# Relative-position attention: relative stores, bias loads and output stores on GpSimd's queue, relative products at a head's last step, transposes three steps behind

## What is computed

```
Q, K, V = x @ Wq.T, x @ Wk.T, x @ Wv.T          # as (b, h, s, 8)
scores = Q K^T / sqrt(8)
dist = clip(k - q, -128, 128) + 128
scores = scores + einsum('bhqd,qkd->bhqk', Q, pek[dist]) / sqrt(8)
scores = where(causal, scores, -inf)
attn = softmax(scores)
out = attn V + einsum('bhqk,qkd->bhqd', attn, pev[dist])
return merged(out) @ Wo.T
```

## Time and profile before

| | us |
|---|---|
| median of 3 runs (4418.83 to 4434.67) | 4421.69 |
| the profiled execution | 4445.3 |
| its span, first to last instruction | 4443.5 |
| TensorE busy in it | 2959.2 (67%) |
| VectorE busy | 2377.8 (54%) |
| ScalarE busy | 1767.3 (40%) |
| GpSimd busy | 809.7 (18%) |

### The profile page before, as it was taken

One profiled execution on the slowest core, in us unless ns is written; L12 is line 12 of the kernel. 1 busy time (PEld: TensorE's weight loads), 2 busy tenths in 40 slices (PEclk: granted clock), 3 DMA queues, 4 the chain that ended last, 5 costly groups with the idle time before them and its releaser, 6 DMA issues. The chain is left out here.

```text
span 4443.5 us, 68068 instructions
## 1 busy us (share of the span) xinstructions
PE 2959.2 (67%) x21547; PEld 1611.6 (36%) x21547; DVE 2377.8 (54%) x4808; ACT 1767.3 (40%) x4259; POOL 809.7 (18%) x1093
## 2 busy tenths in 40 slices
PE   5588734285443678777887577877777630768885
PEld 2344323154332344444444333333333320752221
DVE  4566466454674566666664344445544441137775
ACT  2355412121111455545554244444444300227675
POOL 2100000021001444444442300000000007022220
PEclk9789866587665899999998666666666655879998
DMA  3422110000001000000000477777777514663331
GB/s 112 76 53 50 40 43 0 8 1 6 0 0 43 19 15 18 18 18 17 10 18 9 140 189 188 189 194 194 189 190 197 135 41 142 169 133 53 58 56 38
DMA packets 457690, 340.63 MB, mean 77 GB/s; under 512 B 64351, under 2 KB 418842, under 8 KB 457378
## 3 DMA queue, kind: packets, MB, share of 16 engines
q1 hardware_dynamic: 434562, 302.49, 27.9%
q0 software_dynamic: 11008, 27.28, 2.1%
q10 hardware_dynamic: 11808, 7.08, 0.6%
HBM read 174.71 MB, written 146.81 MB: 72 GB/s over the span
## 5 line engine op out<-in xcount | busy, mean ns | idle before, releaser
L1156 DVE TENSOR_REDUCE a_soft_NM<-a_soft_s_ps 128x2 f32<-128x1024 f32 (+3 forms) x512 | 515.2, 1021 | 235.3 <-PE a_soft_s_ps L1091 133.3
L1190 ACT ACTIVATE a_soft_PTS<-a_soft_st_ps 128x512 f32<-128x512 f32 (+3 forms) x1024 | 458.9, 523 | 173.5 <-PE a_soft_st_ps L1067 101.9
L465 PE MATMUL a_soft_pt_ps<-net_ident,a_soft_PR 128*128 128x128 f32 x1280 | 328.2, 369 | 116.1 <-ACT a_soft_PTS L567 110.4
L613 ACT ACTIVATE a_soft_PR<-a_soft_s_ps,a_soft_least 128x128 f32<-128x128 f32 (+3 forms) x512 | 263.6, 526 | 341.3 <-DVE a_soft_least L588 227.1
L1062 PE MATMUL a_soft_st_ps<-a_soft_QS,a_soft_KS 50*128 50x512 bf16 (+4 forms) x1024 | 263.0, 365 | 72.8 <-ACT a_soft_PTS L1190 40.7
L465 PEld LDWEIGHTS a_soft_pt_ps<-net_ident,a_soft_PR 128*128 128x128 f32 x1280 | 182.7, 180 | 214.7 <-ACT a_soft_PR L613 154.6
L1104 PE MATMUL a_soft_o_ps<-a_soft_PTS,a_soft_VR 128*32 128x512 f32 (+3 forms) x2048 | 249.5, 562 | 0.1
L2212 PE MATMUL f_run_ps<-f_run_WQKV,f_run_HT 128*128 128x512 f32 x384 | 229.5, 689 | 15.5 <-DVE f_run_RS L1433 8.3
L2545 ACT ACTIVATE f_run_PB<-f_run_ps,f_run_MX 128x128 f32<-128x128 f32 x512 | 179.8, 377 | 136.6 <-DVE f_run_MX L2427 136.6
L2350 POOL TENSOR_TENSOR f_run_QK<-f_run_QK,f_run_T 128x512 f32<-128x512 f32 x128 | 163.2, 1275 | 366.4 <-DVE f_run_T L2405 363.9
L569 DVE COPY a_soft_PTS<-a_soft_pt_ps 128x512 f32<-128x512 f32 (+3 forms) x320 | 169.4, 529 | 69.3 <-PE a_soft_pt_ps L465 42.2
(11 more groups left out here) (376 smaller groups left out, 6473.5 us busy)
## 6 DMA issues: line engine op xcount, KB each, us to landing
a_soft_BIAS<-skew_d SPq DMA_DIRECT2D x256, 191.0 KB, 4.2
band_d<-a_soft_PR SPq DMA_DIRECT2D x256, 191.0 KB, 3.7
skew_d<-a_soft_RS SPq DMA_DIRECT2D x128, 256.0 KB, 4.4
a_soft_PB<-band_d SPq DMA_DIRECT2D x128, 256.0 KB, 3.1
f_run_W<-in_L_ffn_w SPq DMA_DIRECT2D x72, 256.0 KB, 2.7
a_soft_QS<-query_rows_d SPq DMA_DIRECT2D x32, 384.0 KB
query_rows_d<-a_proj_PARTS SPq DMA_DIRECT2D x72, 128.0 KB
query_rows_d<-a_proj_PARTS POOLq DMA_DIRECT2D x72, 128.0 KB
```

The lines of the kernel that those rows point to most:

```text
L465: last = pe.transpose(pt_ps[:, slot, kb * P:(kb + 1) * P], PR[:, n % NPR, OFF + kb * P:OFF + (kb + 1) * P], ident[:])
L613: act.activation(PR[:, n % NPR, OFF:OFF + width(j)], s_ps[:, n % 4, 0:width(j)], ACT.Exp, bias=least[:, n:n + 1], scale=-1.0).then_inc(pro ...
L1156: dve.tensor_reduce(NM[:, T % 2, j, p, :], s_ps[:, ring["s", a] % 2, :, 0:width(j)], AX.X, ALU.max, negate=True).then_inc(max_ready, 1)
L1190: act.activation(PTS[:, T % 2, 2 * p + par, kb, q0:S], st_ps[:, e % 3, q0:S], ACT.Exp, scale=scale).then_inc(probs_ready, 1)
```

## The change

The relative store, the bias loads and the output stores move to GpSimd, with the waits that stand ahead of them; SyncE keeps the operand loads and the band. TensorE makes the relative products in step j = 3 instead of j = 0, between the scores and the transposes; ScalarE copies them last in step j = 3 instead of first in j = 1, and no longer issues the output stores. Rows are transposed three steps behind instead of two (`LAG`). The counts of the semaphores follow (`missing`, `before`, `through`).

```diff
@@ relative_heads @@
+    LAG = 3
     def missing(seq, slots):
-        return sum(m < seq and m % 2 in slots for m in (0, 1, 2, 7))
+        return sum(m < seq and m % 2 in slots for m in (0, 1, 2, 3, 7))
     def before(hd, pos):
...
-        return 5 * hd + pos - 4
+        return 5 * hd + pos - 5
@@ sync @@
-            def store_rel(hd, h, visit):
-                sp.wait_ge(rel_copied, hd + 1)
...
-            def load_bias(hd, h, visit):
...
                 for h in range(4):
...
-                    for f, a in ((store_rel, 3), (load_bias, 2)):
-                        if not (final and h + a >= 4):
-                            f(hd + a, (h + a) % 4, qd if h + a < 4 else qd + 1)
                     store_band(hd, h, qd)
@@ gpsimd @@
+            def store_rel(hd, h, visit):
+                pool.wait_ge(rel_copied, hd + 1)
+                if not (isinstance(hd, int) and hd < 4):
+                    pool.wait_ge(bias_loaded[h], 16 * len(BIAS_WINDOWS) * visit)
+                pool.sem_inc(pool_passed, 1)
+                pool.dma_start(diagonal(skew_d, h), RS[:, h, :, :]).then_inc(rel_stored[h], 16)
+            def load_bias(hd, h, visit):
+                pool.wait_ge(rel_stored[h], 16 * (visit + 1))
+                pool.sem_inc(pool_passed, 1)
+                if not (isinstance(hd, int) and hd < 4):
+                    pool.wait_ge(least_ready, 4 * (hd - 3))
+                pool.sem_inc(pool_passed, 1)
+                for r0, n, c0, m in BIAS_WINDOWS:
+                    pool.dma_start(BIAS[r0:r0 + n, h, :, c0:c0 + m], window(skew_d, h, r0, n, c0, m)).then_inc(bias_loaded[h], 16)
...
+                for h in range(4):
+                    hd = 4 * qd + h
+                    if not (final and h >= 2):
+                        load_bias(hd + 2, (h + 2) % 4, qd if h < 2 else qd + 1)
+                    if not (final and h >= 1):
+                        store_rel(hd + 3, (h + 3) % 4, qd if h < 1 else qd + 1)
+                if prev:
+                    store(qd - 1, 1 - u % 2, *((b, u - 1) if u else (b - 1, 3)))
+            def store(qd, sl, b, u):
+                pool.wait_ge(o_copied, qd + 1)
+                for h in range(4):
+                    pool.dma_start(out_d[ds(b, 1), 4 * u + h].rearrange("a r f -> (a r) f"),
+                                   OS[32 * h:32 * h + HD + 1, sl, :]).then_inc(o_stored[sl], 16)
@@ tensor @@
-                    if j == 0 and not (final and h >= 1):
+                    if j == 3 and not (final and h >= 1):
                         uu, hh = (u, h + 3) if h < 1 else ((u + 1) % 4, h - 1)
                         relative(b if h < 1 or u < 3 else b + 1, uu, hh, 4 * qd + h + 3)
...
-                    if n >= 2:
-                        turn(qd, n - 2, h, pos, qd)
+                    if n >= LAG:
+                        turn(qd, n - LAG, h, pos, qd)
                     elif prev:
-                        turn(qd - 1, n + 14, h, pos, qd)
+                        turn(qd - 1, n + 16 - LAG, h, pos, qd)
@@ scalar @@
                     if prev or n >= NPR:
-                        act.wait_ge(pt_ready, before(4 * qd + h - 2, 4 + j))
+                        act.wait_ge(pt_ready, before(4 * qd + h - 2, (5, 6, 7, 9)[j]))
...
-                    if j == 1 and not (isinstance(b, int) and qd == 4 * B - 1 and h >= 1):
-                        copy_rel(4 * qd + h + 3, (h + 3) % 4, qd if h else qd - 1)
...
                     copies(act, 1, qd, sl, n, prev)
+                    if j == 3 and not (isinstance(b, int) and qd == 4 * B - 1 and h >= 1):
+                        copy_rel(4 * qd + h + 3, (h + 3) % 4, qd if h else qd - 1)
...
-                act.wait_ge(o_copied, qd + 1)
-                bb, uu = (b, u - 1) if u else (b - 1, 3)
-                for h in range(4):
-                    act.dma_start(out_d[ds(bb, 1), 4 * uu + h].rearrange("a r f -> (a r) f"),
-                                  OS[32 * h:32 * h + HD + 1, sl, :]).then_inc(o_stored[sl], 16)
```

More of the change, by code:

```diff
@@ L361, in load @@
                     sp.dma_start(t[:, sl, :], src[ds(b, 1), :, u * 4 * S:(u + 1) * 4 * S].rearrange("a p f -> (a p) f")).then_inc(opnd_loaded[sl], 16)
-            def store_rel(hd, h, visit):
-                sp.wait_ge(rel_copied, hd + 1)
-                if not (isinstance(hd, int) and hd < 4):
-                    sp.wait_ge(bias_loaded[h], 16 * len(BIAS_WINDOWS) * visit)
-                sp.dma_start(diagonal(skew_d, h), RS[:, h, :, :]).then_inc(rel_stored[h], 16)
-            def load_bias(hd, h, visit):
-                sp.wait_ge(rel_stored[h], 16 * (visit + 1))
-                sp.sem_inc(sp_passed, 1)
-                if not (isinstance(hd, int) and hd < 4):
-                    sp.wait_ge(least_ready, 4 * (hd - 3))
-                for r0, n, c0, m in BIAS_WINDOWS:
-                    sp.dma_start(BIAS[r0:r0 + n, h, :, c0:c0 + m], window(skew_d, h, r0, n, c0, m)).then_inc(bias_loaded[h], 16)
             def store_band(hd, h, visit):
@@ L397, in _ @@
             load(0, 0)
-            for hd in range(3):
-                store_rel(hd, hd, 0)
-            sp.wait_ge(init_done, 1)
-            for hd in range(2):
-                load_bias(hd, hd, 0)
             def quad(b, u, prev):
@@ L432, in _ @@
             pool.drain()
+            def store_rel(hd, h, visit):
[12 more added lines that the diff above has]
+                    pool.dma_start(BIAS[r0:r0 + n, h, :, c0:c0 + m], window(skew_d, h, r0, n, c0, m)).then_inc(bias_loaded[h], 16)
+            for hd in range(3):
+                store_rel(hd, hd, 0)
+            for hd in range(2):
+                load_bias(hd, hd, 0)
             def quad(b, u, prev):
                 qd = 4 * b + u
+                final = isinstance(b, int) and qd == 4 * B - 1
                 if not (isinstance(b, int) and qd < 2):
@@ L440, in quad, with last @@
                                  vall[:, ds(qd, 1), :, :].rearrange("p a h (j d) -> p (a h) j d", d=HD)).then_inc(vr_ready, 1)
-            batches(quad, lambda: None, pool)
+                for h in range(4):
[11 more added lines that the diff above has]
+                                   OS[32 * h:32 * h + HD + 1, sl, :]).then_inc(o_stored[sl], 16)
+            def last():
+                store(4 * B - 1, 1, B - 1, 3)
+                for o in o_stored:
+                    pool.wait_ge(o, 64 * 2 * B)
+            batches(quad, last, pool)
         def q_blk(sl, h, j):
@@ L528, in last @@
             def last():
[L529 to L530 removed]
+                turn(4 * B - 1, 13, 0, 0, 4 * B)
+                turn(4 * B - 1, 14, 0, 1, 4 * B)
                 turn_band(4 * B - 1, 2, 0, 4 * B)
[L532 removed]
+                turn(4 * B - 1, 15, 0, 3, 4 * B)
+                turn_band(4 * B - 1, 3, 0, 4 * B, 4)
                 for kb in range(NPT):
[L534 removed]
+                    pv(4 * B - 1, 1, kb, (1, -1))
             for hd in range(3):
@@ L641, in last @@
             def last():
-                copy_out(act, 1, 4 * B, 0, 1, 1, 3, 15)
-                copy_out(act, 1, 4 * B, 0, 3, 1, 3, None)
-                store(4 * B - 1, 1, B, 0)
-                for o in o_stored:
-                    act.wait_ge(o, 64 * 2 * B)
+                copy_out(act, 1, 4 * B, 0, 1, 1, 3, 14)
+                copy_out(act, 1, 4 * B, 0, 3, 1, 3, 15)
+                copy_outputs(4 * B - 1, 1, B, 0)
             for hd in range(3):
```

27 lines of the change are left out of this document (12 added, 15 removed).

## The result

The changed kernel takes 4444.7 us at the median (4436.6 to 4458.6, 9 runs) against 4421.7 for the kernel before: 1.0049 of its time, 95% interval 1.0034 to 1.0064, so 23 us or half a per cent slower. The forecast was 4340. The stage is where it is lost: the exponentials took 944.6 us and take 962.9 now, 18.3 us more. (The profiled execution of after, 4436.6 us, is the shortest of its nine and that of before, 4445.3, lies above all of its own, so the two spans differ the other way; what lies outside the stage is 3498.9 us in that of before and 3472.0 in that of after. So stages are compared in the traces and ratios in the runs.)

What follows compares the result with a forecast made beforehand. SyncE's queue was taken to bound the kernel at 29.6 us a quad. Afterwards GpSimd's 26.4 us a quad, 32 times, plus 17 for loop turns gave 862 against 944.6 us, 82 less: 4340 us, range 4260 to 4480.

Steps and rivals of the forecast that it cites:

- SyncE's loop bound the stage and loses its 2.04 us a head: SyncE's queue in the exponentials' stage: its 7.0 to 7.1 us turn falls to about 5.1 us a head.
- well above 17.8 + 7 us: Sign in the profile after: SyncE's band stores wait this long for exponentials, with band loads under 6.8 us apart.
- The engines take 25.7 us a quad without their two waits: TensorE's quad without waits for ScalarE (1.72 us) and operands (1.47), both said to be removed by the change: 25.7 us.
- The lag and the late products cost zero: Three-step lag and moved relative products: zero taken, up to 20 us of gain left in the range.
- Price of GpSimd's issues, 3.0 us for three: GpSimd's relative store and two bias loads per head: 3.0 us, the middle of 1.6 per issue and 4.4 per run.
- The landing, 3.8 us: GpSimd's relative store lands in 3.8 us, 3.4 behind the issue, as only SyncE's band transfers compete.
- Nothing gained: Rival, chance 0.16: SyncE's queue full but not in the way, landings stretch; 4395 to 4445 us, say 4420.
- about 7.3 if only half the stores meet it: GpSimd's loop per head if only half the stores meet the 5.4 us landing; 8.2 at worst.
- GpSimd's loop is longer than SyncE's was: Rival, chance 0.17: issues priced per run make GpSimd's loop 8.0 us a head, 78 us more, 4500 us.
- The lead of 10.4 us against 13.2: Relative product's way from copy to landed bias takes 10.4 us; VectorE wants it two heads later, 13.2 us: enough.
- The clock: Rival, engines and clock, chance 0.22: less idle time raises TensorE's clock, 1 us a quad; about 4285 us.
- The Trainium skill's two rules: Spreading issuing engines saves only issue time, gain near nothing; GpSimd transfer costs 2.0 us plus bytes, 2.6 for the store.

Runs made afterwards that it cites:

- the swapped order and the late band: Changed kernel with GpSimd's relative store ahead of its bias loads and the band transposed in step j = 3 instead of j = 2; 4368.3 us, 0.9863.
- 0.9891: Changed kernel with relative store ahead of bias loads, relative products back in step j = 0, band transposed in j = 3; 4374.0 us.
- 1.0068: Kernel before with relative stores, bias loads and outputs on GpSimd, but early relative products and a lag of two steps; 4501.9 us.
- either cut of bytes: Changed kernel, after four heads moving one block of four: of the band's stores and loads, 4359.0 us, 0.9856; or of the bias loads, 4350.0 us, 0.9835.
- the late band: Alone: changed kernel with only the band transposed in a head's step j = 3 instead of j = 2; 4473.1 us, 1.0103.
- the early products: Changed kernel with only the relative products back in step j = 0, copied in j = 1; 4463.9 us, 1.0076.
- two edits: On the changed kernel: relative store ahead of bias loads alone, 4457.3 us, 0.9977; band transposed in j = 3 alone, 1.0103; both, 0.9863.

## Why the prediction was wrong, point by point

- **SyncE's loop bound the stage and loses its 2.04 us a head: right.** The loop was there, and SyncE now waits for exponentials, which I had named as the sign. I wanted those waits "well above 17.8 + 7 us"; they are 307. But band loads are 7.35 and 7.63 us apart, not under 6.8: the queue is idle, not faster.
- **The engines take 25.7 us a quad without their two waits: not reached.** The kernel with the swapped order and the late band has 891.8 / 32 = 27.9, with bias waits in it. Both waits went (no operand row, no "issue" row), so their causes were rightly named, but the step "both waits have a reason that the change removes", as a gain, fails: the output stores alone gave 0.3% the wrong way, since the time came back as operand wait.
- **The lag and the late products cost zero: borne out on two queues.** Late products help by 0.27% at most on the order of the change and on the swapped one by nothing that the intervals tell (0.9863 against 0.9891), but with one queue they hold up the band. The lag is the only difference between 1.0068 and 1.0076, two ratios that their intervals don't tell apart.
- **Price of GpSimd's issues, 3.0 us for three: too high.** They take 2.0, nearer the end priced per issue (1.6) than that per run (4.4). By itself this would have made the kernel faster than forecast, so it hid 1.0 us of what the other terms were short. I had written that the change loses when the issues cost over 3.8 us; it lost with 2.0.
- **The landing, 3.8 us: the step that failed.** The landing is 5.5 us from the issue's start and 4.7 behind its end, where I had 3.8 and 3.4. The 0.2 "for waits" is 0.74, the time from the landing to the next issue, which no row of before had shown for GpSimd. So the sum 3.4 + 3.0 + 0.2 = 6.6 should have been 4.7 + 2.0 + 0.74 = 7.5: plus 1.3 for the landing, plus 0.5 behind it, minus 1.0 for the issues. 0.9 x 128 = 115 us, about the 105 between 4340 and 4445. I took the store to compete "only" with SyncE's band. It stands right behind 382 KB of bias loads of its own queue, in an order that the diff shows, and meets the band too; cutting either brings it to 4.4 and 4.5, and another place in the queue and in the head to 4.2. And the 3.2 us of the earlier trace rows were SyncE's; GpSimd's own first stores took 4.3.
- **The rivals: both of the losing ones had a part of it.** "Nothing gained" (chance 0.16) had the stretch of the landings, and its range ends at 4445, where the time came. But its "about 7.3 if only half the stores meet it" is near 7.5 by luck: it counts the issues at 3.0, and with the 2.0 measured it is 6.3, so that it took nearly the full stretch and the 0.74. "GpSimd's loop is longer than SyncE's was" (0.17) had the place and the sign: the loop is 7.52 against 7.39 us, (7.52 - 7.39) x 128 is about the 18 us lost in the stage, and VectorE waits for the bias in most heads. Its price, 4.4 us for the issues, was wrong.
- **The lead of 10.4 us against 13.2: wrong.** It took each store to go out when its copy was done. In the order of the change it stands behind the bias load, which waits for the landing of the store ahead. The product copied by 3106.75 us was stored at 3112.87, its bias loads went out at 3119.25, and VectorE's step that needs them started at 3124.40, after 1.29 us of waiting for them: 17.6 us. Whoever had followed that one product through the queue would have seen that the order, not the sum, was wrong.
- **The clock: no part in it.** The granted clock is 0.67 before and 0.66 after; it is 0.69 or 0.70 in the fastest kernels, where TensorE is busy 83 to 85% of the view and not 79%.
- **The Trainium skill's two rules.** The trace of before gives no landing of a store that GpSimd issued. The runs show 4.3 us near the start and 5.5 in the stage, so the fixed cost plus bytes that the Trainium skill gives in DMA: Bandwidth & Descriptors, section Anatomy of one DMA (2.6 us for this store, an estimate), is too short here by 1.7 to 2.9. The section Issuing engines are not separate DMA queues of the same page of the Trainium skill came nearer than my sum, in its outcome: nothing was gained. What the move saved SyncE is indeed the issues, as that section says; but it calls them usually small beside the transfer, and here they are 2.04 us of a loop of 7.1 whose landing is waited for. The runs with the swapped order and the late band reach 0.9863 with the same two queues and the same bytes, so sharing the DMA engines didn't rule out a gain.

**Still open:** why the store lands later from GpSimd than from SyncE even with little beside it; why either cut of bytes takes away the whole stretch; why the late band costs 0.5% while GpSimd's loop binds, and why the store lands 0.2 to 0.3 us later there and with the early products; what a loop turn costs now, which no run singled out.

## What to carry to other kernels

A store whose landing the same queue waits for is a loop, and its length is issues plus landing, plus the time from the landing to the next issue, whichever engine issues; moving it to an idle engine moves the loop. Before such a move, follow one piece of data through the new queue's order, and put what waits for an engine ahead of what waits for a landing, so that the landing passes while the queue waits anyway. When a first limit is taken away, try the next ones together: here two edits were worth 0.7% and minus 0.5% alone, and 1.9% together.

## What the runs showed of the hardware

- GpSimd issues by shape, but far from in proportion: 0.76 us for 128 rows of four runs of 512 B, 0.625 for 64 rows of four runs of 764 B, and 0.52 for an output store (2.07 / 4). SyncE takes 0.39 for the first and about 0.6 for the second.
- The same store of 256 KB lands in 3.2 us from SyncE and 4.3 from GpSimd with little else running, and in 4.4 and 5.5 in the stage, counted from the issue's start: 1.1 us apart both times, 0.4 of it the longer issue. For the query rows in the projection it is the other way round, 3.7 from SyncE and 3.0 from GpSimd.
- GpSimd issues the waiting bias load 0.74 us after the landing that it waits for (0.64 to 0.80 in 125 waits), SyncE a band load 0.17 us after its landing.
- Landings gave way by about a fifth (5.5 to 4.4 and 4.5 us) when three quarters of some other transfers' bytes were taken away, and as far (to 4.2) with all bytes and a DMA share of 0.79, when the store went out ahead of the bias loads and earlier in the head. With the bytes taken away the DMA share in the stage fell from 0.75 to 0.56 and 0.64:

```profile
2570.00:3440.00 870.00, 738.79 (x3960) 376.11 (x3961) 457.27 (x1578) 446.15 (x974) 319.72 (x528) 0.68 0.56 137
```

```profile
2570.00:3440.00 870.00, 747.09 (x4034) 386.70 (x4037) 470.45 (x1580) 444.65 (x978) 299.80 (x529) 0.68 0.64 165
```
